# A graph-attention kernel on one Trainium2 core: the selection of a pass written in two parts

## The reference, cut to what matters

```
xn = layernorm(x)                                  # 6250 nodes, 256 features
for i in 0..2:                                     # three graph-attention layers, 8 heads of 32
    h  = xn @ W[i];  el, er = <h, al>, <h, ar>     # per node and head
    e  = leaky_relu(el[src] + er[dst], 0.2)        # 200000 edges, sorted by dst
    ex = exp(e - m[dst])
    out[v] = sum over edges into v of ex * h[src]  /  sum of ex
    xn = leaky_relu(out + b, 0.01)                 # without the activation after layer 2
x = x + xn + linear_attention(layernorm(x))
x = x + mixture_of_experts(layernorm(x))           # 8 experts, 2 chosen per node
```

## Time and profile before

| what | value |
| --- | --- |
| time, median of 3 | 7243.95 us (7237.48 to 7246.24) |
| the profiled execution: its own time | 7240.56 us |
| its span on the core | 7238.9 us |
| busy: PE, PEld | 5473.8, 4419.5 us |
| busy: POOL, DVE, ACT | 4550.8, 4464.1, 1582.9 us |
| granted TensorE clock, mean | 0.901 of full speed |

### The profile page before, as it was taken

One profiled execution on the slowest core, in us unless ns is written; L12 is line 12 of the kernel. 1 busy time (PEld: TensorE's weight loads), 2 busy tenths in 40 slices (PEclk: granted clock), 3 DMA queues, 4 the chain that ended last, 5 costly groups with the idle time before them and its releaser, 6 DMA issues.

```text
span 7238.9 us, 140830 instructions
## 1 busy us (share of the span) xinstructions
PE 5473.8 (76%) x35030; PEld 4419.5 (61%) x35031; DVE 4464.1 (62%) x9891; ACT 1582.9 (22%) x4669; POOL 4550.8 (63%) x4739
## 2 busy tenths in 40 slices
PE   4566677777776666666767665678888899999999
PEld 2445555565564454555555553456777778888888
DVE  5455566666665555666676765666666665655554
ACT  2000001111110000000000000013344444555554
POOL 0677777777765777777777757777655454444331
PEclk9788888888887788889898987789999999999999
DMA  4555555555544555555555444444433333222221
GB/s 168 175 142 146 146 148 149 150 152 148 144 140 116 142 142 145 144 144 146 147 148 144 139 118 135 140 133 129 118 110 104 93 95 87 83 84 80 73 73 41
DMA packets 386096, 916.18 MB, mean 127 GB/s; under 512 B 130561, under 2 KB 192777, under 8 KB 385930
## 3 DMA queue, kind: packets, MB, share of 16 engines
q0 software_dynamic: 227904, 681.63, 34.8%
q1 hardware_dynamic: 115530, 194.09, 7.9%
q10 hardware_dynamic: 42624, 40.02, 1.6%
HBM read 871.89 MB, written 43.49 MB: 126 GB/s over the span
## 4 chain that ended last, share of the span: by engine, by line
PE 28%; POOL 28%; issue 23%; DVE 8%; DVEq 7%; DMA 3%; ACTq 2%; ACT 2%; POOLq 1%; SPq 0%
POOL gat L411 27%; PE bank L1446 9%; PE bank L1373 9%; PE bank L1362 6%; DVEq L254 2%; DMA gat<-table,meta 2%; DVE msg L1116 2%; ACTq L254 1%; DVE selT L1088 1%; DVE sel L1124 1%; PE bank L1316 1%; DVE lg L1106 1%; ACT L501 1%; DVEq L1142 1%; DVEq L1107 0%
## 5 line engine op out<-in xcount | busy, mean ns | idle before, releaser
L411 POOL DMA_INDIRECT gat<-table,meta x4716 | 4537.5, 962 | 2538.3 <-issue 1366.3
L1446 PE MATMUL bank<-msg,sel 128*128 x10560 | 3174.8, 452 | 1347.2 <-DVE sel L1124 1330.3
L1446 PEld LDWEIGHTS bank<-msg,sel 128*128 128x128 f32 x10560 | 2183.5, 217 | 1810.8 <-issue 1436.9
L1116 DVE SCALAR_TENSOR_TENSOR msg<-bank,gat 128x1056 f32 x1320 | 1658.3, 1256 | 273.9 <-ACT bank L544 250.2
L544 ACT ACTIVATE bank<-lg 128x32 f32<-128x32 f32 x1320 | 262.8, 199 | 4620.5 <-DVE lg L1110 4485.3
L1124 DVE TENSOR_TENSOR sel<-iota_t,meta 128x512 f32<-128x512 f32 x1320 | 903.4, 684 | 93.9 <-PE bank L1446 90.1
L1106 DVE TENSOR_TENSOR lg<-gat,bank 128x64 f32<-128x64 f32 x880 | 193.3, 220 | 999.8 <-POOLq L418 759.3
L1373 PE MATMUL bank<-w,region 128*128 128x256 f32 x3136 | 758.5, 385 | 31.8 <-ACT region L501 31.6
L1362 PEld LDWEIGHTS bank<-xT,w 128*128 128x128 f32 x6272 | 750.5, 192 | 15.8
L1362 PE MATMUL bank<-xT,w 128*128 128x128 f32 x6272 | 759.6, 276 | 0.0
L1416 PEld LDWEIGHTS bank<-uvb,selT 128*128 128x128 bf16 x10584 | 391.3, 98 | 445.7 <-DVE selT L1088 252.8
(11 more groups left out here) (215 smaller groups left out, 2559.5 us busy)
## 6 DMA issues: line engine op xcount, KB each, us to landing
dstb<-dst_lists SPq DMA_DIRECT2D x297, 512.0 KB
gat<-table,meta POOLq DMA_INDIRECT x4716
table<-hrow ACTq DMA_DIRECT2D x98, 140.0 KB, 2.7
w<-in_W SPq DMA_DIRECT2D x2, 4096.0 KB
table<-hrow SPq DMA_DIRECT2D x49, 140.0 KB, 1.8
region<-xnT_d ACTq DMA_DIRECT2D x50, 128.0 KB
region<-qT_d ACTq DMA_DIRECT2D x50, 128.0 KB
res<-in_x SPq DMA_DIRECT2D x1, 6272.0 KB, 25.4
```

What stands on the lines that cost most here:

```text
L411: pool.indirect_dma_start(gat[:, r, c, :], None, table[l], bass.IndirectOffsetOnAxis(meta[:, m, c, 0:1].bitcast(U32), 0)).then_inc(s_done, 16)
L1116: dve_v.scalar_tensor_tensor(msg[:, bass.ds(n % 2, 1), :, :].rearrange("p a c (h d) -> p (a c) h d", h=H), ex_p.unsqueeze(3).to_broadcast( ...
L1446: last = pe.matmul(acc[:, 0:MSG], sel[:, c, :], msg[:, bass.ds(m % 2, 1), c, :].rearrange("p a m -> p (a m)"), start=opens and c == 0, sto ...
```

## The change

`sel` is written by two DVE instructions of 2 chunks each (`HALF = 2`) and not by one of 4. PE aggregates the 2 chunks of the first part after a semaphore of their own (`half_ready`), and the other 2 after the semaphore that used to cover all. PE signals `agg_done` after each part, so it counts two a pass, and `select` waits for each part by itself; `divide` waits for the second. The pass number is multiplied by two in registers (`snap`). Five semaphores of the set-up are folded into two, with the same waits in the same places.

```diff
                 def select(g, n, done):
-                    dve.wait_ge(agg_done[l], n)
-                    dve_v.tensor_tensor(sel[:], iota_t[:].unsqueeze(1).to_broadcast([P, CH, P]),
-                                        meta[:, bass.ds(g % LISTS, 1), :, 1:2].rearrange("p a c w -> p (a c) w").to_broadcast([P, CH, P]),
-                                        ALU.is_equal).then_inc(done, 1)
+                    for half, ready in enumerate((half_ready[l], done)):
+                        at = half * HALF
+                        dve.wait_ge(agg_done[l], dve.snap(2 * n + half))
+                        dve_v.tensor_tensor(sel[:, at:at + HALF, :], iota_t[:].unsqueeze(1).to_broadcast([P, HALF, P]),
+                                            meta[:, bass.ds(g % LISTS, 1), at:at + HALF, 1:2].rearrange("p a c w -> p (a c) w").to_broadcast([P, HALF, P]),
+                                            ALU.is_equal).then_inc(ready, 1)
                 def divide(T, n_next):
-                    dve.wait_ge(agg_done[l], n_next)
+                    dve.wait_ge(agg_done[l], dve.snap(2 * n_next + 1))
-                def aggregate(m, opens=False, closes=False):
-                    for c in range(CH):
-                        last = pe.matmul(acc[:, 0:MSG], sel[:, c, :], msg[:, bass.ds(m % 2, 1), c, :].rearrange("p a m -> p (a m)"),
-                                         start=opens and c == 0, stop=closes and c + 1 == CH)
-                    last.then_inc(agg_done[l], 1)
+                def aggregate(m, whole, count, opens=False, closes=False):
+                    for half, (ready, at_least) in enumerate(((half_ready[l], m), (whole, count))):
+                        pe.wait_ge(ready, at_least)
+                        for c in range(half * HALF, half * HALF + HALF):
+                            last = pe.matmul(acc[:, 0:MSG], sel[:, c, :], msg[:, bass.ds(m % 2, 1), c, :].rearrange("p a m -> p (a m)"),
+                                             start=opens and c == 0, stop=closes and c + 1 == CH)
+                        last.then_inc(agg_done[l], 1)
...
                     pe.wait_ge(acc_free[l], T + 1)
-                    pe.wait_ge(tile_first[l], T + 1)
-                    aggregate(n0, opens=True)
+                    aggregate(n0, tile_first[l], T + 1, opens=True)
...
                             prepare_next(n, T)
-                            pe.wait_ge(slot_done[l], m)
-                            aggregate(n)
+                            aggregate(n, slot_done[l], m)
...
                     prepare_next(n3, T + 1)
-                    pe.wait_ge(tile_last[l], T + 1)
-                    aggregate(n3, closes=True)
+                    aggregate(n3, tile_last[l], T + 1, closes=True)
...
-                dve.sem_inc(agg_done[l], 1)
+                dve.sem_inc(half_ready[l], AHEAD)
+                dve.sem_inc(agg_done[l], 3)
```

More of the change, by code:

```diff
@@ L28 @@
 BATCH = 4
+HALF = 2
 LEAST = 5
@@ L200, in build @@
         x_in, k_in, w_in, d_in, late_in, experts_in = map(sem, ("x_in", "k_in", "w_in", "d_in", "late_in", "experts_in"))
-        ext_ready, var_ready, std_ready, flags_ready, flagsT_ready, slots_ready, sums_ready, ctl_ready = map(
-            sem, ("ext_ready", "var_ready", "std_ready", "flags_ready", "flagsT_ready", "slots_ready", "sums_ready",
-                  "ctl_ready"))
+        ext_ready, var_ready, std_ready, ctl_ready = map(sem, ("ext_ready", "var_ready", "std_ready", "ctl_ready"))
+        step_ready, step_summed = sem("step_ready"), sem("step_summed")
         turn_taken = sem("turn_taken")
@@ L208, in build @@
         ctl_out, ctl_in, zeros_ready = sem("ctl_out"), sem("ctl_in"), sem("zeros_ready")
-        ranges_ready, prev_ready, d16_ready, d16_out = map(sem, ("ranges_ready", "prev_ready", "d16_ready", "d16_out"))
+        d16_ready, d16_out = sem("d16_ready"), sem("d16_out")
         xn_ready, xn_free, xT_psum, xT_ready = map(sem, ("xn_ready", "xn_free", "xT_psum", "xT_ready"))
@@ L216, in build @@
         (meta_in, list_ready, gathered, selT_ready, uv_ready, logit_ready, ex_ready,
-         slot_done, tile_first, tile_last, agg_done, acc_free) = (
+         slot_done, tile_first, tile_last, half_ready, agg_done, acc_free) = (
             [sem(f"{n}{l}") for l in range(LAYERS)] for n in (
@@ L220, in build @@
                 "selT_ready", "uv_ready", "logit_ready", "ex_ready", "slot_done", "tile_first", "tile_last",
-                "agg_done", "acc_free"))
+                "half_ready", "agg_done", "acc_free"))
         xo_ready, xoT_psum, xoT_ready = (
@@ L716, in _ @@
                 dve.drain()
-            dve.sem_inc(flags_ready, 1)
-            dve.wait_ge(flagsT_ready, 1)
+            dve.sem_inc(step_ready, 1)
+            dve.wait_ge(step_summed, 1)
             lf = small[:, 240:244]
@@ L748, in _ @@
             dve.drain()
-            dve_v.tensor_tensor(end, low, held, ALU.add).then_inc(ranges_ready, 1)
-            dve.wait_ge(prev_ready, 1)
+            dve_v.tensor_tensor(end, low, held, ALU.add).then_inc(step_ready, 1)
+            dve.wait_ge(step_summed, 2)
             dve_v.tensor_scalar(rows, low, 1.0, None, ALU.add)
@@ L754, in _ @@
             dve.drain()
-            dve_v.tensor_tensor(rows, held, share, ALU.subtract).then_inc(slots_ready, 1)
-            dve.wait_ge(sums_ready, 1)
+            dve_v.tensor_tensor(rows, held, share, ALU.subtract).then_inc(step_ready, 1)
+            dve.wait_ge(step_summed, 3)
             out_ctl = ismall[0:NT, 16:16 + CTL]
@@ L1281, in _ @@
             pe.wait_ge(k_in, 16)
-            pe.wait_ge(flags_ready, 1)
+            pe.wait_ge(step_ready, 1)
             fl = small[:, 128:128 + 2 * NT].rearrange("p (w t) -> p w t", w=2)
             pe.matmul(tp[0:NT, 0:P], fl[:, 0, :], ident, start=True, stop=True)
[L1286 to L1290, removed]
+            pe.matmul(tp[0:NT, P:2 * P], fl[:, 1, :], ident, start=True, stop=True).then_inc(step_summed, 1)
+            pe.wait_ge(step_ready, 2)
+            pe.matmul(tp[0:NT, 258:259], kc[0:NT, K_PREV:K_PREV + NT], small[0:NT, 238:239], start=True, stop=True).then_inc(step_summed, 1)
+            pe.wait_ge(step_ready, 3)
             held = small[0:NT, 239:242]
@@ L1293, in _ @@
             pe.matmul(tp[0:NT, 263:266], ones[0:NT, 0:NT], held, start=True, stop=True)
-            pe.matmul(tp[0:NT, 266:269], kc[0:NT, K_NEXT:K_NEXT + NT], held, start=True, stop=True).then_inc(sums_ready, 1)
+            pe.matmul(tp[0:NT, 266:269], kc[0:NT, K_NEXT:K_NEXT + NT], held, start=True, stop=True).then_inc(step_summed, 1)
             pe.wait_ge(ctl_ready, 1)
```

## The result

The changed kernel takes 7212.41 us (median of 6 runs, 7205.03 to 7216.21), the kernel before 7244.43 us (median of 6): a ratio of 0.9958, 95% interval 0.9948 to 0.9968. The forecast was 7210 us in a range of 7170 to 7248, so the sum was right to 2 us. The profiled executions have spans of 7238.9 and 7203.6 us, 35.3 us apart.

A forecast was written before the change was run, and what follows sets the result against it. POOL's gathers were taken to bound most earlier stretches and PE the time from 5200 us; 18.7 + 6.2 + 6.9 + 5.1 + 5 - 8 = 33.9 us off the median of 7243.95 gave 7210 us, range 7170 to 7248.

The forecast's parts named there:

- Who bounds what: POOL bounds 2280 to 3900 us and similar stretches, PE from 5200 us on; they share 4800 to 5200 us.
- One sign that it had set itself: Profile after: if the last layer doesn't shorten by 20 to 30 us, the step on who bounds what is wrong.
- The first part of `sel`: PE starts 0.26 us sooner at its waits: 18.7 us after 5200 us, 6.2 us from 4800 to 5200 us.
- POOL: Gathers delayed while `sel` runs: shorter holds if POOL gets in between the parts; 5 us gained.
- the bound of -25: Limit set on the change in POOL's gather delays, from -25 to +10 us, with -5 taken.
- DVE's longer `sel`: Two parts take 0.08 us more; 100 passes on DVE's path at late tile ends and in the last layer: -8 us.
- The waits of `sel` on PE: Late in the second layer, 18 waits of 0.57 us nearly vanish, half on the path: 5.1 us gained.
- the tile starts: Late in the first two layers, PE starts 0.26 us sooner at 43 tiles, less 0.10 us snaps each: 6.9 us.

The follow-up runs named there:

- E1: Against the kernel before: `sel` written by two DVE instructions of two chunks, waits and signals as before; 7272.13 us against 7242.09, ratio 1.0038.
- E3: Against the changed kernel: PE waits for both parts of `sel` before its first chunk; 7263.46 us, ratio 1.0029 to the kernel before.
- E4: Against the changed kernel: two parts in the last layer alone, the first two layers as before; 7219.43 us against 7241.75, ratio 0.9969.
- E5: Against the changed kernel: two parts in the first two layers alone, the last as before; 7227.69 us, ratio 0.9982 to the kernel before.
- E6: Against the changed kernel: a semaphore for each of PE's parts, no doubled pass number; 7197.76 us, ratio 0.9938 to the kernel before.
- E7: Against the changed kernel: `sel` in parts of one and three chunks; 7205.69 us, ratio 0.9951 to the kernel before.
- E8: Against the changed kernel: `sel` in four parts of one chunk, a PE signal after each; 7216.88 us, ratio 0.9963 to the kernel before.
- E9: Against E6: parts of 1 and 3 chunks in the last layer, equal parts in the first two; 7189.78 us, ratio 0.9927 to the kernel before.
- the first set: Four variants, E1, E3 and E6 among them, run on another chip, where the kernel before took 9382.12 us beside E1.

## Why the prediction was right, and where it wasn't

**Who bounds what: right in the main.** The first stretch, which POOL bounds, changed by no more than its gathers' own time, and the last one by PE's waits. PE waits 160 us less for `sel` over the kernel, and the gain is 32 us. After 5200 us these waits are 70, of 96.1 us together, and the forecast had some 72, of about 96. One sign that it had set itself did fail: it called this step wrong if the last layer didn't shorten by 20 to 30 us, and it shortened by 16. By the waits above, the terms were too large there, and who bounds the stretch was not wrong.

**The first part of `sel`: right, a little large.** Forecast 0.26 us at each wait, measured 0.23, and 2.6 us come back as a wait of PE for L948. After 5200 us the sum had 18.7 us; the 64 waits of the last 264 passes gave 12. For 4800 to 5200 us it had 6.2, and the last layer's first 176 passes gave 4.

**POOL: the mechanism right, the size too small.** The forecast took 5 us in all and left open whether two holds in a row let the other in. They do; the hold that the Trainium skill describes (page SBUF — State Buffer, section Who interferes with whom) ends with each instruction, as the gather at 961.47 shows. In the first layer's first 308 passes alone POOL's busy time fell by 8.5 us and the time by 6. All gathers together take 28 us less (4537.5 to 4509.1), just past the bound of -25, but only those in POOL's stretches are time, and in the second layer's first 308 passes nothing was gained (1437 us in both). In all ten kernels of this chip the first stretch is 355 to 358 us longer than POOL's busy time in it, so POOL is its bound throughout. But E1 and E3, with the same halved `sel`, took 1447 and 1444 us there: their gathers met shorter holds too, and lost it again by the 3 ns in the median. So the halving by itself doesn't explain the 6 us in full.

**DVE's longer `sel`: a term without its largest part.** The sum had -8 us for it, 100 passes of 0.08 us on DVE's path. By itself, in E1 at 7240 us, splitting costs 27 us, and with the early start of `sel` but PE waiting for both parts (E3) 21 us. The last stretch pays what the step says, 5 us. The 27 us late in E1's second layer are of another kind: PE's busy time there rises by the same 27 us, at a granted clock of 0.85 and not 0.88. The forecast had no term for the clock. Whether the longer `sel` brings the lower clock about or the two fell together in this trace, no run settles; E4 shows that this stretch can swing by 12 us with its code unchanged. That E1 and E3 are slower in the medians of five and seven executions, with intervals clear of 1, says that the loss itself is no swing.

**The waits of `sel` on PE, and the tile starts: not to be sized one by one.** They were worth 5.1 and 6.9 us in the sum. DVE's waits went, as forecast (90.1 to 14.1 us). Late in the second layer the two terms made 8 us and the stretch gave 15; late in the first they made 4 and it gave nothing. Against E3 the changed kernel is 28 us shorter late in the second layer and 51 in all. The forecast's own steps would give that comparison 0.34 us at 72 + 24 + 43 waits and 5 of waits, which is 52 us, but that the two sums agree is luck: the same prices would have 11 us late in the second layer and 9 late in the first, where the traces have 28 and -1.

**Booked together.** The second layer's last 132 passes in all ten kernels of this chip: their time, PE's busy time in it, and what is left, in us.

| kernel | PE's start | time | PE busy | left |
| --- | --- | --- | --- | --- |
| before | after the whole `sel` | 634 | 428.9 | 205 |
| E1 | after the whole `sel` | 661 | 455.8 | 205 |
| E3 | after the whole `sel` | 647 | 438.6 | 208 |
| E4 | after the whole `sel` | 622 | 416.2 | 206 |
| changed | after the first part | 619 | 427.5 | 192 |
| E5 | after the first part | 630 | 438.4 | 192 |
| E6 | after the first part | 626 | 433.4 | 193 |
| E7 | after one chunk | 623 | 438.5 | 185 |
| E8 | after one chunk | 641 | 453.0 | 188 |
| E9 | after the first part | 632 | 439.9 | 192 |

What is left falls by 12 to 14 us with PE's start after two chunks and by 17 to 21 after one. PE's busy time swings by 40 us between kernels, beside that. So the changed kernel's 15 us here are 13 or 14 of PE's earlier start and 1 of busy time; and E1's longer `sel`, by this reckoning, costs nothing here but the busy time. The subtraction is an argument and not a measurement of its own, since each kernel has one trace; it holds in all ten.

## What to carry to other kernels

A producer cut in two is worth what its consumer can start earlier, and here it was worth something only when the consumer got the signal of the first part: without it the cut cost 0.4% here, with it it gained 0.4%. Count the waits where the consumer is the bound and multiply by the time that the first part saves; the fall of that wait over the whole kernel was five times the gain. Where another engine is held up by the producer's instructions, the length of its instructions is a price of its own. In these traces equal parts suited the stretch that this other engine bounds (1438 to 1443 us against 1452 with parts of one and three), and a short first part the one that the consumer bounds (1943 against 1949). The kernel that chose by layer was 0.7% faster than the one before, but it had other semaphores too, and how much of that the choice gave is not shown.

## What the runs showed of the hardware

In the trace of the kernel before, 286 gathers start while DVE writes `sel`, whose two inputs are in SBUF, and at least 0.15 us before it is done. The 38 that start within 0.04 us of it take their 0.95 us; the other 248 end about 0.82 us after it, and the longest takes 1469 ns. The addition at L1143 and `selT` (L1088) hold gathers in the same way, the latter to 1072 ns at most because it lasts only 0.35 us. The 1080 gathers that start in the same way during `msg`, which is longer (1.26 us) but reads one input from PSUM, take 962 ns at most. Two DVE instructions issued back to back, whose records overlap by 0.08 us, let a gather in between.

An aggregation of 8 records takes 2.04 us or, at some places late in the second layer, 3.62 us or more, after waits of much the same length. Two from the changed kernel's timeline:

```profile
4240.02 2.04 PE L1451 MATMUL bank<-msg,sel 128*128 x8 [1.64 <-DVE sel L1127]
...
4244.25 3.62 PE L1451 MATMUL bank<-msg,sel 128*128 x8 [1.26 <-DVE sel L1127]
```

The granted clock of the second layer's last 132 passes, a mean over its two levels of 1.2 and 2.4 GHz, was between 0.85 and 0.91 over the kernels, and the length of the stretch followed PE's busy time, as the table above shows. Over the 3.62 us of the slow aggregation the granted clock was 0.54, over the fast one 1.00. What decides in which tile the clock is at the lower level was not found.

On the other chip of the first set the same kernel took 30% longer. The variants that ran on both stood in nearly the same order there (E6 ahead of the kernel before, E1 and E3 behind it), but E6's gain was 0.1%, not clear of zero, and not 0.6%.
